# Filler matmuls at four places, bias steps moved, and a closer start in a macaron block kernel

## The reference

```python
x = x + 0.5 * ffn(layernorm(x))     # mixture of experts
x = x + attn(layernorm(x))          # gated complex recurrence and an MLP
x = x + 0.5 * ffn(layernorm(x))     # the same experts again

def ffn(t):                          # 8 experts, capacity 160 rows each
    probs = softmax(t @ gate_w + gate_b); e = argmax(probs)
    pos = running count of rows that chose the same expert
    keep = pos < 160                 # later rows of a full expert get nothing
    h = gelu(t @ w1[e] + b1[e]); out = (h @ w2[e] + b2[e]) * probs[e] * keep

def attn(t):
    q, k, v, g, a = t @ Wq, t @ Wk, t @ Wv, t @ Wg, t @ Wa     # a: real and imaginary half
    a = sigmoid(|a|) * exp(i * angle(a))
    h[s] = a[s] * h[s-1] + k[s] * v[s]                          # complex scan over 1024 rows
    y = layer_norm(real((q * h * silu(g)) @ Wo) + t)
    return layer_norm(gelu(y @ W1 + b1) @ W2 + b2 + y)
```

## Time and profile before

| what | value |
|---|---|
| time, median of three runs | 702.91 us |
| profiled execution, its time | 710.14 us |
| profiled execution, its span | 708.4 us |
| mean granted clock of TensorE | 0.974 |
| TensorE matmul busy | 654.4 us, 92% |
| VectorE busy | 475.7 us, 67% |
| ScalarE busy | 450.6 us, 64% |
| GpSimd busy | 194.8 us, 28% |

### The profile page before, as it was taken

One profiled execution on the slowest core, in us unless ns is written; L12 is line 12 of the kernel. 1 busy time (PEld: TensorE's weight loads), 2 busy tenths in 40 slices (PEclk: granted clock), 3 DMA queues, 4 the chain that ended last, 5 costly groups with the idle time before them and its releaser, 6 DMA issues. The chain is left out here.

```text
span 708.4 us, 11935 instructions
## 1 busy us (share of the span) xinstructions
PE 654.4 (92%) x4510; PEld 576.8 (81%) x4523; DVE 475.7 (67%) x1042; ACT 450.6 (64%) x810; POOL 194.8 (28%) x290
## 2 busy tenths in 40 slices
PE   8889999989998999999999999999998999789993
PEld 7568999465678899798898898898887788589993
DVE  6844500447979989889989989988989876510001
ACT  4224442169699799798899798897797244244440
POOL 6160111220024126126216216215224231500112
PEclk9999999999999999999999999999999999899998
DMA  9979960612011011021022021011011095207700
GB/s 276 322 258 314 376 219 16 179 64 60 31 59 52 25 45 51 26 75 46 31 75 74 1 75 59 17 45 46 1 45 45 3 354 195 58 18 245 253 22 26
DMA packets 53010, 74.10 MB, mean 105 GB/s; under 512 B 4774, under 2 KB 44795, under 8 KB 52952
## 3 DMA queue, kind: packets, MB, share of 16 engines
q1 hardware_dynamic: 48600, 59.84, 26.1%
q0 software_dynamic: 4352, 13.49, 5.3%
HBM read 58.26 MB, written 15.20 MB: 104 GB/s over the span
## 5 line engine op out<-in xcount | busy, mean ns | idle before, releaser
L1639 PE MATMUL bank<-zt_h,w_in_h 128*128 128x512 f32 x192 | 80.0, 417 | 6.2 <-DVE qg L1313 3.5
L1639 PE MATMUL bank<-yt_h,w_h 128*128 128x256 f32 x256 | 74.3, 290 | 6.1 <-DVE yt_l L1423 4.0
L982 PE MATMUL bank<-xdt,ring 128*128 128x160 f32 x512 | 76.7, 309 | 1.2 <-ACT xdt L814 0.6
L1640 PE MATMUL bank<-zt_l,w_in_h 128*128 128x512 f32 x192 | 75.9, 395 | 0.0
L982 PEld LDWEIGHTS bank<-xdt,ring 128*128 128x128 f32 x512 | 73.9, 198 | 2.4 <-issue 2.0
L1641 PE MATMUL bank<-zt_h,w_in_l 128*128 128x512 f32 x192 | 75.5, 393 | 0.0
L787 DVE SCALAR_TENSOR_TENSOR xo<-bank,gate,xg 128x256 f32<-128x256 f32 x20 | 9.2, 481 | 96.9 <-PE bank L1009 96.9
L995 PE MATMUL bank<-hid,ring 128*128 128x160 f32 x512 | 72.8, 300 | 1.5 <-DVE idx_s L771 0.7
L1639 PE MATMUL bank<-w_h,ht_h 128*128 128x256 f32 x256 | 73.7, 288 | 0.0
L995 PEld LDWEIGHTS bank<-hid,ring 128*128 128x128 f32 x512 | 70.4, 190 | 2.3 <-issue 2.3
L1640 PE MATMUL bank<-yt_l,w_h 128*128 128x256 f32 x256 | 72.1, 282 | 0.0
(11 more groups left out here) (252 smaller groups left out, 1634.2 us busy)
## 6 DMA issues: line engine op xcount, KB each, us to landing
ring<-in_L_ffn_w SPq DMA_DIRECT2D x32, 1024.0 KB, 8.3
z_mid<-zb POOLq DMA_DIRECT2D x8, 512.0 KB, 3.4
zr<-z_mid SPq DMA_DIRECT2D x16, 256.0 KB, 2.9
xr<-x_mid SPq DMA_DIRECT2D x16, 256.0 KB, 3.8
out<-xq POOLq DMA_DIRECT2D x16, 256.0 KB, 4.3
zb<-x_mid SPq DMA_DIRECT2D x7, 512.0 KB, 4.9
xc<-in_L_attn_x SPq DMA_DIRECT2D x4, 512.0 KB, 4.7
ring<-in_L_attn_x SPq DMA_DIRECT2D x4, 512.0 KB, 7.7
```

The lines of the kernel that those rows point to most:

```text
L982: ins = T.matmul(bank[b][:, 0:CAP], w1_of(s)[:, k, m * P:(m + 1) * P], xdt[:, k, e * CAP:(e + 1) * CAP], start=k == 0, stop=k == KD - 1)
L1639: T.matmul(out, left[0], right[0], start=start, stop=False)
L1640: T.matmul(out, left[0], right[1], start=False, stop=False)
```

## The change

The diff has five parts.

1. In the first expert stage, the bias tables are turned behind the last group, and ScalarE copies them. The sum of the gate matrix (`gate_sum`) goes to bank 7 and runs in the middle of `row_turn(1)`; the wait for `gate_ready` moves from `row_turn(1)` to `row_gate(0)`.
2. Both expert stages: `keep_busy(5)` before the first `turn_in` becomes 3 (first) and 11 (second); `turn_in(0)` gets 5 (first) or 3 (second) fillers behind it, `turn_in(1)` 2. In the second stage, ten fillers between `count` and `list_tokens` become seven.
3. `z_low`: the bias rows are prepared behind `zt_l` instead of before it.
4. `wo`, first quarter of blocks 1 to 6: three (block 1) or five fillers ahead of the wait for `yo`.
5. `up` of block 1, first call: six fillers, with a wait that keeps them from a buffer still being read.

```diff
--- before.py
+++ after.py
@@ -717,12 +717,9 @@
             if first:
                 row_stats(0)
                 v.wait_ge(made, 1)
-                v.wait_ge(bt_ready, 1)
-                own.step(V.tensor_copy(cst["b1t"][:], bank[4][:, 0:NE * KF]))
-                V.tensor_copy(cst["b2t"][:], bank[4][:, NE * KF:NE * (KF + KD)]).then_inc(bt_done, 1)
                 v.wait_ge(sum_ready, 1)
                 zeros = NB // 2 * NE - NE
-                own.link(V.scalar_tensor_tensor(cst["gate_c"][:], bank[5][:, 0:NE].unsqueeze(1).to_broadcast([P, KD, NE]),
+                own.link(V.scalar_tensor_tensor(cst["gate_c"][:], bank[7][:, 0:NE].unsqueeze(1).to_broadcast([P, KD, NE]),
                                                 -1.0 / D, cst["gate_w"][:], ALU.mult, ALU.add))
                 V.tensor_copy(gate_wide[:, :, zeros:zeros + NE], cst["gate_c"][:]).then_inc(gate_ready, 1)
                 for n in range(1, NB):
@@ -802,6 +799,9 @@
                     if n == NB // 2:
                         raw_logits(0)
                 raw_logits(1)
+                act.wait_ge(bt_ready, 1)
+                S.activation(cst["b1t"][:], bank[4][:, 0:NE * KF], ACT.Copy).then_inc(bt_done, 1)
+                S.activation(cst["b2t"][:], bank[4][:, NE * KF:NE * (KF + KD)], ACT.Copy).then_inc(bt_done, 1)
             for b, ts in enumerate(routes):
                 act.wait_ge(shifted, b + 1)
                 e = slice(ts[0] * NE, ts[1] * NE)
@@ -832,6 +832,8 @@
                                  bias=cst["b2t"][:, e * KD + d:e * KD + d + 1]).then_inc(eo_done, 1)
 
             do = dict(turn_in=turn_in, up=up, down=down)
+            if first:
+                act.wait_ge(bt_done, 2)
             for name, n in expert_steps():
                 if name in do:
                     do[name](n)
@@ -844,18 +846,28 @@
                     pe.wait_ge(x_in[n], 16)
                     if n >= 2:
                         pe.wait_ge(xt_ready, KD * (n - 1))
-                    if n == 1:
-                        pe.wait_ge(gate_ready, 1)
                     for d in range(KD):
+                        if n == 1 and d == 1:
+                            gate_sum()
                         for j in range(JT):
                             ins = T.transpose(bank[4 * (n % 2) + d][:, j * P:(j + 1) * P],
                                               xc[n][:, j, d * P:(d + 1) * P], ident[:])
                         ins.then_inc(tp_ready, 1)
 
+                def gate_sum():
+                    pe.wait_ge(made, 1)
+                    pe.wait_ge(gp_in, 64)
+                    for k in range(KD):
+                        ins = T.matmul(bank[7][:, 0:NE], cst["ones"][:], cst["gate_w"][:, k, :], start=k == 0,
+                                       stop=k == KD - 1)
+                    ins.then_inc(sum_ready, 1)
+
                 def row_gate(n):
 
                     b, i = divmod(n, NB // 2)
                     pe.wait_ge(xt_ready, KD * (n + 1))
+                    if n == 0:
+                        pe.wait_ge(gate_ready, 1)
                     at = (NB // 2 - 1 - i) * NE
                     for k in range(KD):
                         for j in range(JT):
@@ -921,15 +933,6 @@
                     T.matmul(bank[3][:, 0:P], cst["ones_h"][:], cst["ones_h"][:], start=True, stop=True)
                 pe.wait_ge(ident_made, 1)
                 row_turn(0)
-                pe.wait_ge(made, 1)
-                pe.wait_ge(gp_in, 64)
-                T.transpose(bank[4][:, 0:NE * KF], cst["eb"][:], ident[0:NE * KF, 0:NE * KF])
-                T.transpose(bank[4][:, NE * KF:NE * (KF + KD)], cst["eb2r"][:],
-                            ident[0:NE * KD, 0:NE * KD]).then_inc(bt_ready, 1)
-                for k in range(KD):
-                    ins = T.matmul(bank[5][:, 0:NE], cst["ones"][:], cst["gate_w"][:, k, :], start=k == 0, stop=k == KD - 1)
-                ins.then_inc(sum_ready, 1)
-                pe.wait_ge(bt_done, 1)
                 for n in range(1, NB):
                     row_turn(n)
                     if n == NB // 2 + 1:
@@ -937,6 +940,9 @@
                     row_gate(n - 1)
                 row_gate(NB - 1)
                 row_back(1)
+                T.transpose(bank[4][:, 0:NE * KF], cst["eb"][:], ident[0:NE * KF, 0:NE * KF])
+                T.transpose(bank[4][:, NE * KF:NE * (KF + KD)], cst["eb2r"][:],
+                            ident[0:NE * KD, 0:NE * KD]).then_inc(bt_ready, 1)
                 pe.wait_ge(made, 2)
                 keep_busy(14)
                 count(0, routes[0])
@@ -953,11 +959,11 @@
                 yield
                 keep_busy(1)
                 count(1, routes[1])
-                keep_busy(10)
+                keep_busy(7)
                 list_tokens(routes[1])
                 keep_busy(4)
                 list_rows(rows[1])
-            keep_busy(5)
+            keep_busy(3 if first else 11)
 
             def turn_in(a):
                 pe.wait_ge(gxn_ready, a + 1)
@@ -969,6 +975,10 @@
                     ins = T.transpose(bank[6 + a % 2][:, d * P:(d + 1) * P], xn[:, a % XB, d * P:(d + 1) * P],
                                       ident[:])
                 ins.then_inc(gtp_ready, 1)
+                if a == 0:
+                    keep_busy(5 if first else 3)
+                if a == 1:
+                    keep_busy(2)
 
             def up(e):
                 s = e % GE
@@ -1283,6 +1293,10 @@
 
 
             def z_low(b, j):
+                for k in range(KD):
+                    v.wait_ge(zh_ready, b.n * KD + (k + 1))
+                    V.tensor_tensor(zt_l[:, k, :], proj[k][:], zt_h[:, k, :].bitcast(F32),
+                                    ALU.subtract).then_inc(proj_read[k], 1)
                 if is_first(b):
 
                     v.wait_ge(par_in, 16 * 6)
@@ -1293,10 +1307,6 @@
                     own.link(V.tensor_copy(b2_up[32:33, :], b2_raw[32:33, :]))
                     own.link(V.tensor_tensor(b2_hl[32:33, :], b2_raw[32:33, :], b2_up[32:33, :].bitcast(F32),
                                              ALU.subtract))
-                for k in range(KD):
-                    v.wait_ge(zh_ready, b.n * KD + (k + 1))
-                    V.tensor_tensor(zt_l[:, k, :], proj[k][:], zt_h[:, k, :].bitcast(F32),
-                                    ALU.subtract).then_inc(proj_read[k], 1)
 
             def fold(b, j):
                 h, i = divmod(j, 3)
@@ -1706,8 +1716,10 @@
                 if is_first(b) and q == 0:
                     hidden_bias()
                     keep_busy(18, o_attn)
+                wait(pe, o_attn_read, quarter_no)
+                if 0 < b.n < NB - 1 and q == 0:
+                    keep_busy(3 if b.n == 1 else 5, o_attn)
                 pe.wait_ge(yg_done, b.n * 2 + 2)
-                wait(pe, o_attn_read, quarter_no)
                 for t in range(QT):
                     c = slice((q * QT + t) * P, (q * QT + t + 1) * P)
                     for k in range(KD):
@@ -1727,6 +1739,9 @@
 
             def up(b, j):
                 q, m = divmod(j, KF // 2)
+                if b.n == 1 and j == 0:
+                    pe.wait_ge(gelu_done[0], b.n * 4)
+                    keep_busy(6, upb[0])
                 if m == 0:
                     pe.wait_ge(yt_ready, KD * (b.n * 2 + q + 1))
                 wait(pe, gelu_done[m % 2], b.n * 4 + (2 * q + m // 2))
```

## The result

The changed kernel takes 696.27 us (median of five runs, 695.24 to 699.1), and the kernel before, beside it, 703.67 us (702.84 to 707.9). The ratio is 0.990, with a 95% interval of 0.9866 to 0.9934. I forecast 697.0 us. A ratio here compares the fast executions of the two kernels and isn't the quotient of the two medians beside it, from which it departs by up to 0.4%. They gave 0.9997 and 0.9868, so the first ratio isn't the whole story.

A forecast was written before the change was run, and what follows sets the result against it. TensorE was 92% busy, so time could come only from its waits and half-clock stretches. Gains of 8.1 us less losses of 2.15 us, net 5.95 us, took 702.9 to 697.0 us (forecast's own range 695.5 to 699; overall 692.5 to 702.3).

The forecast's parts named there:

- Projections: Output projections of blocks 2 to 6: five fillers remove three clock falls, 5.0 us gained; blocks 3 and 5 lose 0.2 us.
- Block 1's three: Three fillers at block 1's output projection, with no wait there to cover them: 0.65 us lost.
- third rival: Block 1's fillers find cover under a wait for `yo` and the first stage brings 1.6 us: 695.05 us, chance 0.18.
- The six ahead of the MLP: Six fillers before block 1's first MLP matmul, with nothing to absorb them: 1.3 us lost (bounds 0 and 1.5).
- First stage: First expert stage's new order: logits earlier, 0.8 us gained, the middle of 1.6 and 0, since a new clock fall was possible.
- Fillers around `turn_in`, first stage: Fillers around the first `turn_in`s of the first expert stage lie in waits for gathered rows: nothing gained or lost.
- Second stage: Second expert stage: 1.1 us gained by three fewer fillers before `list_tokens`, 1.2 us by full clock in the first `up`.
- Bias step behind `zt_l`: Bias step in `z_low`: the 0.52 us wait for `zt_l` goes, but the stop at `qg` takes it back, 0 gained.
- The 7.2 us between the profile and the median of before: Unprofiled median 702.91 us against 710.14 us profiled, unexplained; the predicted net gain of 5.95 us was taken over unchanged.
- The slower one: Rival: timed runs have no falls at the projections, so only the fillers' costs remain: 705.05 us, chance 0.10.
- The first rival: Only the projections pay; both expert stages give 0 as falls move to neighbouring thin stretches: 700.05 us, chance 0.17.
- The clock falls in spite of fillers: Rival: the falls at the three projections stay despite the fillers: 702.0 us, chance 0.10.

The follow-up runs named there:

- six instead of ten: Changed kernel with six instead of ten fillers between first stage's `list_tokens` and `list_rows`, and without the six before block 1's first MLP matmul: 703.25 us, ratio 0.9943 to the kernel before.
- all that helped: Changed kernel without block 1's nine fillers and those around the first `turn_in`s, six instead of ten before first stage's `list_rows`: 698.98 us, ratio 0.9911 to the kernel before.

## Why the prediction was right, and where it wasn't

**Projections.** Right. Five fillers remove the falls: none of the nine profiles that have them shows one at a projection of blocks 2 to 6. A block with the fall avoided goes from 53.54 to 51.83 us, and the cost in blocks 3 and 5 is nil instead of 0.1 us each (51.71 against 51.87 us). "Three are 5.0 us" is right for the profile read and too much for the mean run: the four further profiles without these fillers fell at two, two, one and two of the three. Alone they gave 3.8 us.

**Block 1's three.** Priced at 0.65 us on the path. The cover named in the third rival comes and goes with the fall at 228. Of the six profiles with these three fillers, two don't have that fall and wait 0.31 and 0.32 us behind them; four have it (at 223 to 227) and don't wait. No run takes out the three alone.

**The six ahead of the MLP.** Predicted 1.3 us, measured 1.0 us on the first chip. Taking all nine out gave 1.7 us on the second, against 1.95 forecast. I found nothing that they hold up: the clock in block 1 and at block 2's projection held without them.

**First stage.** The step that moved the logits was right: 21.85 where 21.7 was forecast, with GpSimd last; the gate matmuls of group 0 at 8.60 where 8.5 was. So was the doubt: the wait ahead of `count` grew to 1.93 us, and a fall behind `list_tokens` took the gain back in that profile. It is the rule more than the exception: seven of the ten profiles with the new order have a fall at 32 to 34 us. With the old order, the three that fall at 8 to 9 us don't have it, and the one that doesn't fall there has it at 34. So one fall was mostly exchanged for another, and the middle of 0.8 us was generous for the executions profiled. What I didn't see is another limit, the weights of the second expert, which I had not looked up: in two profiles whose first `up` came at 40.3 the second one waited 1.25 and 1.91 us for them.

On the rule weighed there, the Trainium skill, "TensorE: Matmul & The Clock Gate", Part 4 (PE-mode transpose): by it the half clock that began at 9.7 would have stayed. It is gone in all ten profiles with the new order, and three of the four with the old order have one beginning between 8 and 10 us. So the trace speaks against that use of the rule, though no run isolates transposes. The start of the logits doesn't tell the two apart (21.8 by the rule, 21.7 without it, 21.85 measured), since GpSimd is the last there.

**Fillers around `turn_in`, first stage.** Wrong in size: "nothing gained or lost (bounds 0 and 0.3 lost)". They cost 1.0 us from the transposes to the first `up`, since the rows of both groups were ready together and the five fillers stand between them. I priced them against the old spacing of the two groups in the profile of before, where TensorE waited for each.

**Second stage.** `list_tokens` came directly behind seven fillers: 10.78 us ahead of before (596.60 against 607.38), having been 9.69 ahead at `count` just in front of it (593.76 against 603.45), so 1.1 us as forecast. But that gain needs the half clock. "Gone in any case" was wrong: where the clock held, `list_tokens` waits 0.85 us behind the seven for `hot` (at 601.38, 597.18 and 597.51 in the profiles with six instead of ten, without the fillers around `turn_in`, and with all that helped), and three fillers at 0.22 us would have fitted into that wait. The first `up` gave 1.8 us where 1.2 was said. I had taken 5.18 us for an `up` at full clock; it takes 4.58 where ScalarE follows at once, and in the profile of before it didn't. On the second chip the fillers around the first `turn_in`s of both stages are worth 2.2 us in the median.

**Bias step behind `zt_l`.** The wait of 0.52 us is gone. That the next stop, at `qg`, takes it back is argued and not shown, since no run has this step alone.

**The 7.2 us between the profile and the median of before.** "I can't tell what those are" was the weak place. The profile of before has the late signals too: ScalarE activates in steps of up to 1.8 us in both first `up`s, and 5.6 us of its waits are "remote". The time of 702.91 us and this profile may not belong to one state of things. Taking the absolute difference over was right by luck as much as by reason: of two effects that my sum didn't hold, falls that come in some executions only made it too large, and the better first `up`s made it too small. How much each weighed no run shows. On the first chip the changed kernel took 706.1 us, outside my range; on the second 696.9.

**The rivals.** The slower one (705.05 us, only the fillers' costs remain) would seem to fit the first chip's 706.1 us, but its mechanism isn't what the runs show there: the fillers at the projections pay on that chip too (0.9947 alone), and the loss stands in the two first `up`s. The first rival, in which falls move to neighbouring thin stretches, is near the truth for the first stage. "The clock falls in spite of fillers" is out by the nine profiles.

What stays open: why TensorE's signals come late, or seem to, on one chip, and why the changed kernel loses more by them (706.1 against 696.9, 9 us) than the kernel before (706.3 to 707.9 against 704.4, 2 to 3.5 us). There is no profile of the kernel before from the second chip, and an edit that removes the late signals wasn't tried.

## What to carry to other kernels

Fillers under a wait that recurs at one place cost nothing and pay on the average of the executions; fillers where no wait follows cost their full time, and between two groups that are ready together they delay the second. Before you price a gain at the start of a stage, look up when the next loaded operand lands, since that load may already be the limit. Repeat a comparison of 1% on a second chip before you believe it, and look at whether the profile that you reason from belongs to the same state as the times.

## What the runs showed of the hardware

- Falls of the granted clock are not a property of the program alone, though some places recur. Three profiles of the same changed program all have one at 33, one at 180 to 186 and one at 593 to 599 us; the first has no other ahead of the end, the second three more (46, 227, 616), the third two (49, 223). Without fillers the same gaps of 1.6 us ahead of three projections brought three, two, two, one and two falls in five profiles, not at the same places.
- A fall at a projection cost the block 1.6 to 1.7 us wherever it began: with 2.58 us for the eight output matmuls the block took 53.48 us, with 3.58 us 53.54 us, and without a fall 51.7 to 51.9 us. The time of the eight alone (1.99 us is usual) doesn't tell the price. The first `up` took 6.36 or 6.55 us with a fall where 4.58 is usual.
- On one chip, while the DMA engines were busy for the whole time with weights (share 1.0 and above from 42 us on, as on the other), ScalarE went on up to 3.3 us after the transposes it waited for, and then for the most part in steps of 1.4 to 2.2 us (the longest 4.4 us, in the run of the expert stages' fillers alone). From 36 to 56 us there is one packet on an instruction queue in each of the profiles (0.9 to 1.7 us), with late signals and without, so it isn't the number of instruction loads there. The cause stays open.
